# Two more waits inside GpSimd's row of gathers in a graph attention kernel on one core

## The chip, the core and the metric

The kernel runs on one core of a Trainium2 chip. The metric is the device time of one execution in microseconds (us); lower is better. The core has five engines that run side by side and meet through semaphores: TensorE (PE), VectorE (DVE), ScalarE (ACT), GpSimd (POOL) and SyncE (SP).

## The reference

Two layers of graph attention over a graph of 12500 nodes and 200000 edges, with the edges sorted by destination, and a self loop at each node:

```python
def _gat_layer(h_in, W, a_s, a_d, b, src, dst, n):
    h = (h_in @ W).reshape(n, Hh, Cc)                  # 4 heads x 64 channels
    alpha_s = jnp.sum(h * a_s, axis=-1)
    alpha_d = jnp.sum(h * a_d, axis=-1)
    e = jax.nn.leaky_relu(alpha_s[src] + alpha_d[dst], 0.2)
    m = jax.lax.stop_gradient(jax.ops.segment_max(e, dst, num_segments=n))
    ex = jnp.exp(e - m[dst])
    alpha = ex / jax.ops.segment_sum(ex, dst, num_segments=n)[dst]
    out = jax.ops.segment_sum(h[src] * alpha[:, :, None], dst, num_segments=n)
    return out.reshape(n, Hh * Cc) + b
...
h = jnp.maximum(_layernorm(x, axis=-1), 0.0)
h = gelu(_gat_layer(h, W0, ...)); h = gelu(_gat_layer(h, W1, ...))
return x + h
```

## The kernel before

A dense first part (up to about 170 us) normalises x, multiplies it by W0 and stores a table of rows in DRAM: for each node 264 numbers, four heads of 64 channels and two logits. It also lays the edge list out in chunks of 14 x 128 edges and works out on the chip how many steps there are.

The rest is 112 steps for each of the two layers, 224 in all. A step takes one chunk of 1792 edges and one window of 128 destination nodes. Its work is spread over five bodies of a software pipeline, so in each body five neighbouring steps are under way, each in another role:

- **GpSimd** brings the source rows of a step: 14 gathers (13 in the first 68 steps, where ScalarE makes the last column itself), each an indirect DMA of 128 rows of 1056 bytes into one column of the tile `rows_all` (buffer u of 4, L598 before the change). In front of a step's gathers it waits for `sum_done` of the step three before (L594) and for the step's edge list, `edge_landed` (L595). One group of instructions like this is one step for GpSimd; nothing else is on its queue after the dense part.
- **VectorE**, once a step's rows have landed (`landed`), copies the logits out (`take_values`, L1091), scans for maxima along the edges, and joins the scans across partitions with a carry from step to step (`scan_partitions`; the last operation, L1122, signals `carry_ready`). In the same body it finishes falls and weights of the step before (L1170 to L1183, L1081), compares edge destinations with the window to make one-hots (`one_hots_of_edges`, L1106, which signals `onehot_ready`), and finishes the nodes of the step two before (`node_shares`, `node_totals`, `node_means` up to L1201).
- **TensorE** turns carries round (L1321), spreads logits to edges (L1310) and sums the weighted rows by destination: `sum_up`, 14 products of 128x128 by 128x264 in fp32 (L1328; each stands as two passes, 28 rows of the trace a step). The last of them signals `sum_done`.
- **ScalarE** makes exponentials, weighs the last columns and stores results; **SyncE** loads edge lists, destination rows, marks and the nodes' own rows.

The order on each engine is written out by hand: the function `pipeline` calls the engine's body for each step, and semaphores that count steps hold the engines together. `t.done(1)` is the count that a semaphore has when the step before t is through; `t.done(3)` the one for three steps before. `nc.gpsimd.sem_inc(gathers_begun, 1)` only gives the wait an instruction to hang on.

Of the kernel before, what the change touches and what calls it, by code (L numbers as in the profile page):

```python
# [23 lines left out]
def two_layer_graph_attention(nc, x, src, dst, edge_attr, W0, a_src0, a_dst0, b0, W1, a_src1, a_dst1, b1, out):  # L24
# [44 lines left out]
    with ExitStack() as ctx:  # L69
# [3 lines left out]
        def sem(name):  # L73
            return ctx.enter_context(nc.semaphore(name))
# [184 lines left out]
        gathers_begun, aggr_begun, loads_begun = sem("gathers_begun"), sem("aggr_begun"), sem("loads_begun")  # L259
# [32 lines left out]
        s = {n: sem(n) for n in step_sems}  # L292
# [181 lines left out]
        def _(pool):  # L474
# [107 lines left out]
            for L in range(2):  # L582

                if L == 0:
                    pool.wait_ge(rows_stored[0], 16 * (GROUPS // 2 + 2))
                    pool.wait_ge(rows_stored[1], 16 * (GROUPS // 2))
                else:
                    pool.wait_ge(stored, (rounds_ + 1) * (16 * NB) + 16)
                    nc.gpsimd.sem_inc(gathers_begun, 1)
                def gather_round(r, counts, slots):  # L590
                    for u in range(NB):
                        t = Step(pool, L, r, rounds_, u, counts, slots < SLOTS)
                        pool.wait_ge(s["sum_done"], t.done(3))
                        pool.wait_ge(s["edge_landed"][u], t.landed(16))  # L594
                        nc.gpsimd.sem_inc(gathers_begun, 1)  # L595
                        index = edge[u][:, E_SRC, :].bitcast(I32)
                        for j in range(slots):
                            nc.gpsimd.indirect_dma_start(  # L598
                                out=G[u][:, j, :], out_offset=None, in_=table[L][0:N, :],
                                in_offset=bass.IndirectOffsetOnAxis(ap=index[:, j:j + 1], axis=0)).then_inc(s["landed"][u], 16)  # L600

                if L == 0:
                    with nc.gpsimd.Fori(0, AHEAD) as r:
                        gather_round(r, {}, SLOTS - 1)
                with nc.gpsimd.Fori(AHEAD if L == 0 else 0, rounds_ + 1) as r:
                    gather_round(r, {}, SLOTS)
# [815 lines left out]
```

## Time and profile before

| what | value |
|---|---|
| median of 3 runs (lowest, highest) | 4977.21 us (4950.52, 4978.08) |
| the profiled execution | 4959.4 us |
| its span in the trace | 4957.5 us |
| granted TensorE clock, mean over the span | 0.76 |
| first gather of a step, first and last step | 169.8 us and 4897 us |

The trace is of one execution, 1.9 us longer than its span. In it an instruction row of GpSimd's gathers is the time in which the engine makes the transfer's descriptors; the data lands later. "Idle before" on a row is the time in which the engine had nothing to show, with what the profile names as its end: "issue" is nothing that it sees, "remote" a semaphore whose giver it can't name. Waits, register operations and semaphore operations are not counted as busy and don't stand in the timeline; the view by source line has them.

### The profile page before, as it was taken

To read this page: it belongs to the slowest core of one execution; us is meant where nothing else is said; L and a number is where in the kernel's file an instruction comes from. 1 tells how busy PE (TensorE), PEld (TensorE's weight loads), DVE (VectorE), ACT (ScalarE), POOL (GpSimd) and SP (SyncE) were. 2 spreads that over 40 slices of the span, in tenths; PEclk is the share of its full clock that TensorE was granted. 3 is DMA by queue.
4 is the path that set the end of the run, shared out by engine and by line. 5 is a ranking of instruction groups with operands and counts; after the bars stand their busy time and mean duration, and the time that the engine had idled before them with its cause. 6 is when DMAs were issued, how large, how long until landed. Compare 5 with 4: busy or idle time off the path is not lost.

```text
span 4957.5 us, 58322 instructions
## 1 busy us (share of the span) xinstructions
PE 2920.6 (59%) x10195; PEld 1927.3 (39%) x10195; DVE 3692.9 (74%) x13203; ACT 2353.5 (47%) x7376; POOL 3054.6 (62%) x3215
## 2 busy tenths in 40 slices
PE   7467666677666555565545555555555555555555
PEld 6244444444444333343423333333333333333333
DVE  7577777878777677676757777777777777777777
ACT  5255555555555444444443444444444444444445
POOL 7566656666656655566546666666666666666664
PEclk9688888888788777777767777777777777777777
DMA  8444444444444444444434444444444444444443
GB/s 266 141 129 128 128 119 128 132 128 126 125 120 127 124 115 123 117 121 122 122 99 124 128 133 133 133 133 132 133 135 133 132 130 133 133 133 131 134 135 91
DMA packets 326730, 645.75 MB, mean 130 GB/s; under 512 B 97683, under 2 KB 195387, under 8 KB 326635
## 3 DMA queue, kind: packets, MB, share of 16 engines
q0 software_dynamic: 152224, 428.76, 32.5%
q1 hardware_dynamic: 128664, 172.56, 11.5%
q10 hardware_dynamic: 45746, 43.56, 2.6%
q14 instruction: 85, 0.69, 0.0%
q8 instruction: 11, 0.18, 0.0%
HBM read 596.90 MB, written 47.71 MB: 130 GB/s over the span
## 4 chain that ended last, share of the span: by engine, by line
DVE 70%; issue 14%; another core or an unknown queue 11%; PE 2%; ACT 1%; DVEq 1%; POOL 1%; DMA 0%; ACTq 0%; SPq 0%; POOLq 0%
DVE rows_all L1081 9%; DVE groups_or_hots L1106 9%; DVE stores_or_hots L1059 5%; DVE of_node L1162 3%; DVE vectors_or_means L1201 3%; DVE total L1188 3%; DVE node_logit L1160 3%; DVE node_l L1152 2%; DVE runs L1117 2%; DVE dloc L1103 1%; DVE stats_or_carry L1122 1%; DVE runs L1119 1%; DVE logit L1180 1%; DVE pre L1178 1%
## 5 line engine op out<-in xcount | busy, mean ns | idle before, releaser
L598 POOL DMA_INDIRECT rows_all<-table,edge x3068 | 2933.2, 956 | 1821.5 <-issue 953.7
L1328 PE MATMUL bank<-rows_all,groups_or_hots 128*128 128x264 f32 x6272 | 1783.3, 440 | 47.3 <-issue 23.0
L1328 PEld LDWEIGHTS bank<-rows_all,groups_or_hots 128*128 128x128 f32 x6272 | 1328.9, 219 | 452.6 <-issue 147.2
L1310 PE MATMUL bank<-stores_or_hots,logit_p 128*128 128x448 bf16 x896 | 368.8, 566 | 1314.6 <-DVE logit_p L1072 1142.0
L706 ACT ACTIVATE rows_all<-rows_all 128x64 f32<-128x64 f32 x3584 | 881.6, 341 | 3.7
L1310 PEld LDWEIGHTS bank<-stores_or_hots,logit_p 128*128 128x128 bf16 x896 | 98.9, 131 | 1513.0 <-DVE logit_p L1072 1214.7
L1081 DVE TENSOR_TENSOR rows_all<-rows_all,bank 128x768 f32<-128x768 f32 (+1 forms) x672 | 658.8, 1037 | 0.0
L1106 DVE TENSOR_TENSOR groups_or_hots<-bank,dloc 128x1792 f32<-128x1792 f32 x224 | 453.5, 2025 | 159.5 <-remote 101.2
L736 ACT ACT_TABLE_LOAD x224 | 287.4, 1283 | 400.2 <-issue 377.6
L718 ACT ACTIVATE share<-node_d 128x8 f32<-128x8 f32 x224 | 47.0, 210 | 694.5 <-DVE node_d L1155 550.7
L730 ACT ACTIVATE bank<-fall 128x56 f32<-128x56 f32 x224 | 49.6, 222 | 544.2 <-DVE fall L1183 357.8
L1201 DVE SCALAR_TENSOR_TENSOR vectors_or_means<-normed_or_dst,inv,bias 128x64 f32<-128x64 f32 x896 | 195.9, 281 | 145.3 <-remote 82.7
L1059 DVE TENSOR_SCALAR stores_or_hots<-normed_or_dst,node 128x448 bf16<-128x448 int16 x896 | 252.5, 342 | 50.4 <-remote 40.9
L730 ACT ACT_TABLE_LOAD x222 | 284.8, 1283 | 4.7 <-ACT row L744 0.7
L1315 PE MATMUL bank<-ident,ahead 128*4 128x128 f32 x224 | 81.9, 366 | 291.8 <-issue 167.6
L724 ACT ACTIVATE bank<-products_or_rows,share 128x64 f32<-128x64 f32 x896 | 233.5, 331 | 0.0
L1336 PE MATMUL bank<-total,heir 128*128 128x264 f32 x448 | 226.7, 606 | 0.8 <-DVE heir L1189 0.8
L721 ACT ACTIVATE vectors_or_means<-bank,share 128x65 f32<-128x65 f32 x896 | 209.2, 317 | 7.3
L736 ACT ACTIVATE bank<-vectors_or_means 128x256 f32<-128x256 f32 x112 | 43.4, 388 | 302.8 <-DVE vectors_or_means L1201 268.6
L1350 PE MATMUL bank<-w_ext,stores_or_hots 128*128 128x264 f32 x448 | 133.4, 423 | 84.1 <-ACT rows_all L699 44.3
L1315 PEld LDWEIGHTS bank<-ident,ahead 128*4 128x4 f32 x224 | 18.7, 83 | 420.4 <-issue 268.1
L1162 DVE TENSOR_REDUCE of_node<-node_logit 128x112 f32<-128x336 f32 x224 | 166.7, 744 | 11.2 <-DVE node_logit L1160 2.8
(192 smaller groups left out, 4054.9 us busy)
## 6 DMA issues: line engine op xcount, KB each, us to landing
normed_or_dst<-dst_row SPq DMA_DIRECT2D x224, 448.0 KB
rows_all<-table,edge POOLq DMA_INDIRECT x3068
products_or_rows<-table SPq DMA_DIRECT2D x224, 132.0 KB
table<-row ACTq DMA_DIRECT2D x112, 132.0 KB
early_or_lists<-in_x_dram SPq DMA_DIRECT2D x112, 128.0 KB
out_dram<-vectors_or_means ACTq DMA_DIRECT2D x112, 128.0 KB
table<-stores_or_hots ACTq DMA_DIRECT2D x24, 528.0 KB
groups_or_hots<-in_x_dram SPq DMA_DIRECT2D x24, 512.0 KB
```

What stands on the lines that cost most here:

```text
L598: nc.gpsimd.indirect_dma_start(out=G[u][:, j, :], out_offset=None, in_=table[L][0:N, :], in_offset=bass.IndirectOffsetOnAxis(ap=index[:, j ...
L706: last = nc.scalar.activation(G4[t.u][:, j, h, 0:C], G4[t.u][:, j, h, 0:C], ACT.Copy, scale=G4[t.u][:, j, h, C:C + 1])
L724: last = nc.scalar.activation(own_part[:, h, :], self_row[t.u][:, h * HW:h * HW + C], ACT.Copy, scale=share[:, 0, h:h + 1])
L730: nc.scalar.activation(edge_w.rearrange("p (t h) -> p h t", h=H), fall[:], ACT.Exp).then_inc(s["w_ready"], 1)
L736: nc.scalar.activation(act_o[t.half][:] if t.L == 0 else act_p, mean_o[:], ACT.Gelu).then_inc(s["act_ready"], 1)
L1059: last = nc.vector.tensor_scalar(flat[:, of], dst_b[t.half][:, of], node[:, 0:1], None, ALU.is_equal)
L1081: nc.vector.tensor_tensor(rows[:, :, 0:C], rows[:, :, 0:C], wide(edge_w[:, t0 * H:t1 * H], 2, C), ALU.mult).then_inc(s["weighted"][nth], 1)
L1106: nc.vector.tensor_tensor(onehot[t.half][:], wide(numbers, 1, SLOTS), wide(dloc[:], 2, P), ALU.is_equal).then_inc(s["onehot_ready"], 1)
L1162: nc.vector.tensor_reduce(of_node[:].rearrange("p k h t -> p (k h) t"), node_logit[:].rearrange("p (t c) -> p t c", c=SQ)[:, :, 0:6 * H].r ...
L1201: last = nc.vector.scalar_tensor_tensor(out=mean_o[:, h * C:(h + 1) * C], in0=summed[:, h, :], scalar=inv[:, h:h + 1], in1=bias[:, t.L, h ...
L1310: last = nc.tensor.matmul(bank[0][:, 0:SLOTS * SQ], logit_p[:, q * P:(q + 1) * P], of[:, q], start=(q == 0), stop=(q == QUADS - 1))
L1328: last = nc.tensor.matmul(bank[3 + t.half][:, 0:ROW], onehot[t.half][:, j, :], G[t.u][:, j, :], start=(j == 0), stop=(j == SLOTS - 1))
```

## The change

Inside a step's row of gathers, GpSimd waits twice more: in front of the 10th gather (j == 9) until VectorE has made the carries of the step before, and in front of the 13th (j == 12) until it has made the edge one-hots of the step before. Both hold in all 224 steps. Nothing else is changed, and no other engine has another instruction.

```diff
                         nc.gpsimd.sem_inc(gathers_begun, 1)
                         index = edge[u][:, E_SRC, :].bitcast(I32)
                         for j in range(slots):
+                            if j == 9:
+                                pool.wait_ge(s["carry_ready"], t.done(1))
+                                nc.gpsimd.sem_inc(gathers_begun, 1)
+                            if j == 12:
+                                pool.wait_ge(s["onehot_ready"], t.done(1))
+                                nc.gpsimd.sem_inc(gathers_begun, 1)
                             nc.gpsimd.indirect_dma_start(
                                 out=G[u][:, j, :], out_offset=None, in_=table[L][0:N, :],
                                 in_offset=bass.IndirectOffsetOnAxis(ap=index[:, j:j + 1], axis=0)).then_inc(s["landed"][u], 16)
```

GpSimd's queue over one step of 13 gathers and the start of the next, before the change (x12 means twelve such instructions in a row):

```order
L594 ISA [waits sum_done]
L598 DMA rows_all<-table,edge 128x264 [waits edge_landed0]
L598 DMA rows_all<-table,edge 128x264 x12
L593 REGISTER_ALU
L598 DMA rows_all<-table,edge 128x264 [waits sum_done,edge_landed1]
```

The same place after it:

```order
L594 ISA [waits sum_done]
L604 DMA rows_all<-table,edge 128x264 [waits edge_landed0]
L604 DMA rows_all<-table,edge 128x264 x8
L599 REGISTER_ALU
L604 DMA rows_all<-table,edge 128x264 [waits carry_ready]
L604 DMA rows_all<-table,edge 128x264 x2
L604 DMA rows_all<-table,edge 128x264 [waits onehot_ready]
L593 REGISTER_ALU
L604 DMA rows_all<-table,edge 128x264 [waits sum_done,edge_landed1]
```

No gather has moved against another one; the row of 13 (or 14) is now cut into 9, 3 and 1 (or 2), and the gathers' line number went from 598 to 604.

## Rows read from the trace of the kernel before

**Rows 1.** The page: span, busy times, the chain that ended last

```profile
span 4957.5 us, 58322 instructions
...
PE 2920.6 (59%) x10195; PEld 1927.3 (39%) x10195; DVE 3692.9 (74%) x13203; ACT 2353.5 (47%) x7376; POOL 3054.6 (62%) x3215
...
DVE 70%; issue 14%; another core or an unknown queue 11%; PE 2%; ACT 1%; DVEq 1%; POOL 1%; DMA 0%; ACTq 0%; SPq 0%; POOLq 0%
```

**Rows 2.** Source line 598 from 2600 to 4900 us; idle: us, times

```profile
L598 POOL DMA_INDIRECT rows_all<-table,edge x1527: 943/949/1547, 2599.7 to 4897.8; - x191
...
  issue: 455.4, 1418
  remote: 383.7, 109
```

**Rows 3.** Stages: GpSimd's gathers, busy us (count), clock, from 2600 to 4900 us

```profile
2600.00:4900.00 2300.00, 1459.93 (x1527) 0.72 0.47 132
```

**Rows 4.** Source line 598 from 250 to 1550 us

```profile
L598 POOL DMA_INDIRECT rows_all<-table,edge x845: 943/949/1545, 249.3 to 1542.3; - x169
```

**Rows 5.** Source line 598 from 1550 to 2500 us

```profile
L598 POOL DMA_INDIRECT rows_all<-table,edge x602: 943/949/1218, 1551.9 to 2497.4; - x151
```

**Rows 6.** Timeline of GpSimd, one step: start us, us, [idle before]

```profile
3592.98 0.95 POOL L598 DMA_INDIRECT rows_all<-table,edge  x1 [3.58 <-remote]
...
3604.26 0.95 POOL L598 DMA_INDIRECT rows_all<-table,edge  x1 [0.30 <-issue]
...
3608.02 0.94 POOL L598 DMA_INDIRECT rows_all<-table,edge  x1 [0.30 <-issue]
3609.27 0.94 POOL L598 DMA_INDIRECT rows_all<-table,edge  x1 [0.30 <-issue]
3613.88 0.95 POOL L598 DMA_INDIRECT rows_all<-table,edge  x1 [3.67 <-remote]
```

**Rows 7.** Timeline of TensorE, the end of the sum awaited there

```profile
3604.85 3.38 PE L1328 MATMUL bank<-rows_all,groups_or_hots 128*128 128x264 f32 x14
```

**Rows 8.** Source line 593 (the register operation behind the last gather), same step

```profile
L593 POOLq ALU_OP  x1: 32/32/32, 3599.1 to 3599.1; - x1
```

**Rows 9.** Source line 595 (the second step's wait), from 170 to 180 us

```profile
L595 POOLq EVENT_SEMAPHORE  x1: 43/43/43, 175.4 to 175.4; - x1
```

**Rows 10.** Timeline of GpSimd, the first four steps

```profile
184.84 0.95 POOL L598 DMA_INDIRECT rows_all<-table,edge  x1 [0.30 <-issue]
186.09 0.94 POOL L598 DMA_INDIRECT rows_all<-table,edge  x1 [0.30 <-issue]
...
249.27 0.95 POOL L598 DMA_INDIRECT rows_all<-table,edge  x1 [30.89 <-PE bank L1328]
```

**Rows 11.** Timeline of VectorE in the step of rows 6

```profile
3597.56 0.21 DVE L1091 COPY value<-rows_all 128x56 f32<-128x56 f32 x1
...
3602.26 0.41 DVE L1122 TENSOR_TENSOR stats_or_carry<-runs,lists_or_marks 4x256 f32<-4x256 f32 x1
...
3608.55 2.02 DVE L1106 TENSOR_TENSOR groups_or_hots<-bank,dloc 128x1792 f32<-128x1792 f32 x1 [1.81 <-remote]
```

**Rows 12.** Timeline of GpSimd, the last gather of layer 2's first step

```profile
2580.88 0.95 POOL L598 DMA_INDIRECT rows_all<-table,edge  x1 [0.30 <-issue]
```

**Rows 13.** Timeline of VectorE, the read that waits for that gather

```profile
2583.65 0.21 DVE L1091 COPY value<-rows_all 128x56 f32<-128x56 f32 x1 [17.05 <-DMA rows_all<-table,edge]
```

**Rows 14.** Groups of VectorE, 2600 to 4900 us: busy, mean ns | idle before

```profile
L1106 DVE TENSOR_TENSOR groups_or_hots<-bank,dloc 128x1792 f32<-128x1792 f32 x109 | 220.7, 2025 | 106.7 <-remote 71.6 <-DVE dloc L1103 21.8 <-issue 12.3
```

**Rows 15.** Timeline of VectorE in layer 1 at a loop's turn

```profile
1996.67 0.27 DVE L1170 TENSOR_TENSOR reach<-edge,bank 128x112 f32<-128x112 f32 x1 [4.30 <-issue]
```

**Rows 16.** Timeline of VectorE, the first two steps

```profile
228.97 0.41 DVE L1122 TENSOR_TENSOR stats_or_carry<-runs,lists_or_marks 4x256 f32<-4x256 f32 x1
229.56 2.02 DVE L1106 TENSOR_TENSOR groups_or_hots<-bank,dloc 128x1792 f32<-128x1792 f32 x1
...
236.70 0.20 DVE L1091 COPY value<-rows_all 128x56 f32<-128x56 f32 x1
241.35 0.41 DVE L1122 TENSOR_TENSOR stats_or_carry<-runs,lists_or_marks 4x256 f32<-4x256 f32 x1
```

## The prediction

> **What bounds the kernel now.** I read the page first. VectorE is 74% busy, GpSimd 62%, and the chain that ended last lies 70% on VectorE and 1% on GpSimd [rows 1]; that looks like a kernel bound by VectorE. The source line of the gathers tells another story. From 2600 to 4900 us GpSimd ran 1527 gathers, busy 1459.9 us [rows 3]; its idle time in front of them was 455.4 us in 1418 pieces and 383.7 us in 109 pieces [rows 2]. Together that is 2299.0 of the stretch's 2300 us: gathers and the two kinds of gap fill GpSimd's time. 1527 gathers are 109.1 steps of 14, so a step takes 21.09 us there. It is made of 14 gathers at 0.95 us with 0.30 us between two [rows 6], 17.5 us, a gap between two steps of 383.7 / 109 = 3.52 us in place of one 0.30, which gives 20.8, and some 0.25 us of rarer hiccups in the "issue" pieces. In the first 68 steps (13 gathers) a step takes 1300 us / 65 = 20.0 us [rows 4]; the same sum gives 13 x 1.25 + 3.2 = 19.5. From 1550 to 2500 us a step takes 950 / 43 = 22.1 us [rows 5], a full us over the sum: there VectorE sets the pace, with idle stretches such as 4.30 us in front of L1170 where its loop turns [rows 15].
>
> So the gap of 3.52 us matters more than the page says. What is it? In one step the last gather ends at 3609.27 + 0.94 = 3610.21, and the next step's first starts 3.67 us later [rows 6]. The sum it waits for ended at 3604.85 + 3.38 = 3608.23 by TensorE's rows [rows 7], two us before the gathers were through. A wait tested when its gather's turn comes would have passed for 0.30. The register operation written behind the step's last gather ran at 3599.1, 6.1 us after the first gather started, with nine gathers still to come [rows 8, 6]: GpSimd's sequencer hands out a gather each 6.1 / 14 = 0.44 us and stands at the next wait some 11 us before the queue is empty. At the program's start the semaphores are already high enough. There the second step's wait passed at 175.4, inside the first step's gathers [rows 9], and the gap between the two steps was 0.30 us [rows 10]. I read from this: **a wait that is met when the sequencer reaches it costs nothing; one that is unmet, even if it is met soon after, costs 3.2 us** (3.52 - 0.30), because the next gather then starts only some 3.5 us after the queued ones have ended.
>
> **The change part by part.** Both waits are priced in the step of [rows 6], counted from its first gather (3592.98).
>
> The wait for carries. Nine gathers are handed out in 9 x 0.44 us, less the 0.8 by which the sequencer leads the first one: it stands at the wait at about +3.2. The carries of the step before were done at 3602.67, which is +9.7 [rows 11]. Could they be done by +3.2? VectorE reads a step's logits 2.8 us after its last gather's start at the earliest [rows 12, 13], and carries come 5.1 us after that read (3597.56 to 3602.67) [rows 11]. With the smallest gap between steps, 0.30, the last gather starts at -1.25, so the carries are never there before +6.6. This wait is unmet in every step but the first of a layer: the 9th gather ends at +11.0, the 10th starts at +14.4 in place of +11.3. Price 3.2 us a step. Queued behind it are five gathers and the next step; waiting for these is VectorE's L1091 alone.
>
> The wait for one-hots. Three gathers later, at +13.7 + 3 x 0.44 = +15.0, the sequencer stands here. The one-hots were done at 3610.57, +17.6 [rows 11], in a step with 1.81 us idle in front of L1106; on average that idle is 106.7 / 109 = 1.0 us [rows 14]. That step would miss it. But VectorE has room to be earlier: it reads the logits at +4.6, and the bound above is +1.6. If it runs 3 us earlier, the one-hots come at +14.6 even there, and the wait is met.
>
> The old wait at the step's end. It used to be reached 11 us early. Now the sequencer gets there at +13.7 + 5 x 0.44, about +16. The sum for the next step ended at 3608.23, +15.3 [rows 7], and comes no later if VectorE is earlier. So it is met, and its 3.2 us **fall away**.
>
> The net of a step is 3.2 + 0 - 3.2: one unmet wait before, one after, in another place, 20.8 us before the hiccups as now. The third wait is the doubtful one: bounds are 0 (always met) and 3.2 us (always unmet); below nothing it can't go, since it takes no gather away. I take 0 because one miss shifts GpSimd 3.2 us later against VectorE, and the next step then meets it. Where VectorE sets the pace (22.1 us) a miss hides in the spare time.
>
> At the ends the cover is missing. Step 1's 10th gather used to run at 197; now it waits for carries at 229.38 and its 13th for one-hots at 231.58, unmet, so its data is there at about 240 in place of the read at 236.70 [rows 16]: +3.2. Step 2 starts at about 238, its 9th gather ends at 249.4, then 3.5 us and four gathers: the fourth step's first gather moves from 249.27 [rows 10] to about 258, +9 us in a stretch that GpSimd bounds. Layer 2's second and third steps, back to back today, lose 3.2 us each; a later wait for the sum may take up all of it or nothing (0 to 6), and since it follows within a step I take 2. Sum: 4957.5 + 9 + 2 = 4968.5 us of span, 4970 with the 1.9 us around it. The profiled execution is 18 us under the median of the runs, so on their scale it is 4977 + 11 = **4988 us**.
>
> A page weighed. In [rows 6] the gap stood although the sum was done two us before. The Trainium skill, GPSIMD Engine Reference, Instruction dispatch, says that completion gates what waits on an instruction's semaphore and does not hold back the next Pool instruction. By it a wait would cost only its lateness: carries at +9.7 are before the 10th gather's old turn (+11.3), so the change would cost nothing there; the row speaks against the rule as a price of waits.
>
> **The rivals.**
>
> *VectorE is held less, faster.* VectorE stands idle in front of small operations while GpSimd has gathers queued and stands at a wait, 1.0 us a step before L1106 alone [rows 14]. If a queue cut into 9, 3 and 2 shortens such stretches, what the steps take over GpSimd's sum comes back: 1.0 us of 22.1 in 43 steps [rows 5] and 0.5 of 20.0 in 65 [rows 4], 43 + 32 = 75 us. With the 11 of the ends: 4913 us; if the hiccups of 0.25 us go too (some 180 steps, 45 us), 4868. I take the middle, 4890. Against it: GpSimd's floor of 20.8 us stays. A page tells of such holding: by the Trainium skill, SBUF — State Buffer, Who interferes with whom, a VectorE operation with two SBUF inputs contends with GpSimd reads, one with at most one SBUF input outside the 2-port modes does not. L1106 reads one input in PSUM and waits 106.7 us all the same [rows 14], so the row and the rule differ, and I take no gain from it.
>
> *The one-hots are late in a share of the steps, slower.* It decides at one point: one-hots later than +15.0. The step of [rows 11] is 2.6 us over it. If VectorE, stalled in the stretch before GpSimd's release (now +3 to +13.7 instead of the step's last ten us), doesn't get earlier, the miss returns each time it has slipped again. One step in three: 75 x 3.2 = 240 us, 5228 us; one in eight 5080, two in five 5275.
>
> *Late in nearly every step, slower.* VectorE's own pace then rises with the stalls, to the 24.0 us of two unmet waits. 224 x 3.2 = 717: 5705 us. For it: scans and falls (L1091 to L1183) would stand in the stretch where idle now is. Against: a step of 24 us gives VectorE 3 us to catch up.
>
> *The waits do nothing.* Both met whenever reached: then the step's end pays as before, 4977 us. The bound of +6.6 against +3.2 speaks against it; it would fall into the first case's range.
>
> **How the numbers follow.** The first case, with the last one in it, 0.40, 4940 to 5025 us; faster 0.25, 4860 to 4925; a share of misses 0.20, 5050 to 5290; nearly all 0.15, about 5700. The likeliest gives 4988. The range has to leave out no more than 0.2: it goes from 4860 to 5290 and leaves out the double miss, and a little below and between. A measurement of this kernel tells some 1% from no change, 50 us (its runs spread by 28). Faster by more: 0.25; within: 0.39; slower by more: 0.36.
>
> **What would show it.** In the changed profile the gap between steps is 0.30, and one of 3.4 to 3.6 stands in front of each 10th gather: right for the first part. Gaps over 3 us in front of 13th gathers count the misses: 0 to 30 for the forecast, some 75 for the third case. VectorE's L1091 sits 1.6 to 3 us after the first gather of the next step, not 4.6. If the 10th gather starts at +11.3 in most steps, my price of an unmet wait is wrong; if the gaps stand in front of first gathers as well, the sum for the next step is late, and the time is over 5700. If VectorE's idle in front of L1106 falls below 0.5 us and the middle stretch under 21.5 us a step, the faster rival holds.

## The result and the profile after

The changed kernel takes **5104.16 us** (median of 4 runs, 5090.66 to 5112.16) beside 4977.65 us for the kernel before (4 runs, 4950.52 to 4979.86): a ratio of **1.0268**, 95% interval 1.0234 to 1.0301. The forecast was 4988 us, so 116 us too low. The time lies in the range, in the part that the rival "the one-hots are late in a share of the steps" had brought in; what happened is another thing than that rival, as shown below. The profiled execution has a span of 5096.4 us against 4957.5 [rows 1].

The page of the changed kernel: span and busy times, and the chain that ended last (shares of the span).

```profile
span 5096.4 us, 58882 instructions
...
PE 2903.2 (57%) x10195; PEld 1924.7 (38%) x10195; DVE 3705.3 (73%) x13203; ACT 2347.7 (46%) x7376; POOL 3041.2 (60%) x3215
...
DVE 70%; issue 14%; another core or an unknown queue 12%; PE 1%; POOL 1%; DVEq 1%; DMA 0%; ACT 0%; SPq 0%; ACTq 0%; POOLq 0%
```

VectorE is busy 12 us longer than before, the other engines are not; the page says nothing of where 139 us went. The source line of the gathers (now 604), from 2600 to 5030 us, does. Idle: us, times.

```profile
L604 POOL DMA_INDIRECT rows_all<-table,edge x1496: 943/949/1121, 2600.1 to 5026.1; - x187
...
  DVE groups_or_hots L1112: 568.9, 102
  issue: 410.1, 1345
  remote: 17.0, 5
  DVE stats_or_carry L1128: 13.4, 44
```

The 383.7 us in 109 gaps between steps [rows 2] are down to 17.0 in 5. The 102 pieces that VectorE's L1112 ends are new: 5.6 us each in front of the 13th gather, where the one-hots are awaited. The wait for the carries is named at 44 pieces of 0.30 us, the ordinary distance of two gathers. 2430 us for 1496 / 14 = 106.9 steps make 22.7 us a step, in place of 21.09.

The same line in layer 1's two stretches, for [rows 4] and [rows 5]:

```profile
L604 POOL DMA_INDIRECT rows_all<-table,edge x853: 942/949/1226, 249.8 to 1549.1; - x171
...
  issue: 247.4, 758
  remote: 162.2, 48
  DVE groups_or_hots L1112: 44.1, 20
  PE bank L1334: 24.2, 10
...
L604 POOL DMA_INDIRECT rows_all<-table,edge x600: 943/949/1182, 1549.1 to 2470.8; - x150
```

Here the kernel is faster: 853 gathers of 13 a step are 65.6 steps in the 1300 us that held 65, and 600 gathers (42.9 steps) now fit into 922.6 us, 21.5 us a step for 22.1. By the gathers' timeline layer 2's first gather starts at 2518.2 us for 2564.6 before, and the last step's first gather at 5035.1 for 4897.8. So the ledger is: layer 1 gives 46.4 us back, 111 steps of layer 2 cost 2516.9 - 2333.2 = 183.7 us, the tail 1.6, together 138.9. Of layer 1's 46.4 us, 10.8 are there when the fourth step begins (238.50 in place of 249.27).

A step of layer 2 in GpSimd's timeline, beside [rows 6]:

```profile
3595.70 0.95 POOL L604 DMA_INDIRECT rows_all<-table,edge  x1 [0.30 <-issue]
...
3605.73 0.95 POOL L604 DMA_INDIRECT rows_all<-table,edge  x1 [0.30 <-DVE stats_or_carry L1128]
3606.99 0.95 POOL L604 DMA_INDIRECT rows_all<-table,edge  x1 [0.30 <-issue]
...
3609.49 0.95 POOL L604 DMA_INDIRECT rows_all<-table,edge  x1 [0.30 <-issue]
3616.38 0.95 POOL L604 DMA_INDIRECT rows_all<-table,edge  x1 [5.93 <-DVE groups_or_hots L1112]
```

Count the rows: with the first gather at 3595.70, the one at 3605.73 is the 9th and the one at 3606.99 the 10th, the one that waits. The sequencer passed that wait at 3605.44, as the 8th gather ended, and the view names the carries at the next gather that started. Both stand 0.30 us behind the gather before them. The 13th is the one at 3616.38.

And what VectorE did in between, beside [rows 11] (L1128 makes the carries, L1112 the one-hots; L1137 to L1161 are `node_shares`):

```profile
3604.99 0.41 DVE L1128 TENSOR_TENSOR stats_or_carry<-runs,lists_or_marks 4x256 f32<-4x256 f32 x1
...
3605.87 0.16 DVE L1148 TENSOR_TENSOR least_max<-old_max,products_or_rows 128x4 f32<-128x4 f32 x1
3607.31 0.16 DVE L1150 TENSOR_TENSOR edge_max<-mean_max,absent 128x4 f32<-128x4 f32 x1 [1.28 <-DVE mean_max L1146]
...
3609.41 0.17 DVE L1153 TENSOR_TENSOR total<-edge_max,least_max 128x4 f32<-128x4 f32 x1 [1.87 <-remote]
...
3611.52 0.17 DVE L1156 TENSOR_TENSOR node_z<-total,products_or_rows 128x4 f32<-128x4 f32 x1 [1.83 <-remote]
3612.94 0.17 DVE L1158 SCALAR_TENSOR_TENSOR node_l<-node_z 128x12 f32<-128x12 f32 x1 [1.25 <-DVE node_z L1156]
...
3613.54 2.02 DVE L1112 TENSOR_TENSOR groups_or_hots<-bank,dloc 128x1792 f32<-128x1792 f32 x1
```

The first seven operations after the carries follow each other in 0.1 us. In the program these small operations wait for each other through semaphores. From here on each such wait takes 1.25 to 1.87 us: L1146 ended at 3605.95, and the trace has the rise of its semaphore at 3607.28. So it goes on until the last stall ends at 3612.94: 2.5 us after the last queued gather, 3609.49 + 0.95 = 3610.44. Only then come the one-hots. GpSimd holds back its 13th gather for the one-hots, and the one-hots, behind this chain, come only after GpSimd's queue has run dry. That is the circle.

### The profile page after: what moved, and what is told of

It reads as the page before. It is cut to its first block, busy times and chain, and to the rows that moved or that the text cites. A ratio compares the mean times of both kernels' runs of the same rounds, so it can differ in the third digit from the quotient of the medians.

```text
span 5096.4 us, 58882 instructions
## 1 busy us (share of the span) xinstructions
PE 2903.2 (57%) x10195; PEld 1924.7 (38%) x10195; DVE 3705.3 (73%) x13203; ACT 2347.7 (46%) x7376; POOL 3041.2 (60%) x3215
## 4 chain that ended last, share of the span: by engine, by line
DVE 70%; issue 14%; another core or an unknown queue 12%; PE 1%; POOL 1%; DVEq 1%; DMA 0%; ACT 0%; SPq 0%; ACTq 0%; POOLq 0%
DVE rows_all L1087 9%; DVE groups_or_hots L1112 9%; DVE stores_or_hots L1065 5%; DVE of_node L1168 3%; DVE vectors_or_means L1207 3%; DVE node_logit L1166 2%; DVE total L1194 2%; DVE node_l L1158 2%; DVE runs L1123 2%; DVE node_z L1156 2%; DVE dloc L1109 2%; DVE stats_or_carry L1128 1%; DVE runs L1125 1%; DVE edge_max L1150 1%
## 5 line engine op out<-in xcount | busy, mean ns | idle before, releaser
L1334 PE MATMUL bank<-rows_all,groups_or_hots 128*128 128x264 f32 x6272 | 1776.4, 439 | 48.6 <-issue 22.7
L1112 DVE TENSOR_TENSOR groups_or_hots<-bank,dloc 128x1792 f32<-128x1792 f32 x224 | 453.5, 2024 | 79.2 <-DVE dloc L1109 42.3
L1207 DVE SCALAR_TENSOR_TENSOR vectors_or_means<-normed_or_dst,inv,bias 128x64 f32<-128x64 f32 x896 | 195.5, 280 | 116.0 <-remote 65.6
L1156 DVE TENSOR_TENSOR node_z<-total,products_or_rows 128x4 f32<-128x4 f32 x224 | 37.2, 166 | 224.8 <-remote 211.9
L1158 DVE SCALAR_TENSOR_TENSOR node_l<-node_z 128x12 f32<-128x12 f32 x224 | 38.4, 171 | 205.7 <-remote 109.6
```

The lines of the kernel that those rows point to most:

```text
L1112: nc.vector.tensor_tensor(onehot[t.half][:], wide(numbers, 1, SLOTS), wide(dloc[:], 2, P), ALU.is_equal).then_inc(s["onehot_ready"], 1)
L1207: last = nc.vector.scalar_tensor_tensor(out=mean_o[:, h * C:(h + 1) * C], in0=summed[:, h, :], scalar=inv[:, h:h + 1], in1=bias[:, t.L, h ...
L1334: last = nc.tensor.matmul(bank[3 + t.half][:, 0:ROW], onehot[t.half][:, j, :], G[t.u][:, j, :], start=(j == 0), stop=(j == SLOTS - 1))
```

## The experiments

The first four ran on one chip, with the kernel before beside them at 4977.44 us (7 runs). Diffs are against the changed kernel unless said otherwise.

### Each wait alone

```diff
-                            if j == 12:
-                                pool.wait_ge(s["onehot_ready"], t.done(1))
-                                nc.gpsimd.sem_inc(gathers_begun, 1)
```

> Of the two waits only the one in front of the 10th gather (carries) is kept. Theory on record (R: each wait that is unmet when GpSimd's sequencer reaches it costs 3.2 us): carries' wait 3.2 us, and the wait at the step's end, reached at about +12 against a sum at +15.4, another 3.2 us: 24 us a step, about 5500 us. Theory A (the 10th gather waits only for what its data is late; the loss of the change comes from the one-hots' wait alone, which closes a circle in layer 2): the gap before the 10th gather stays at 0.3 us in most steps, the gap between steps is back at 3.5 us, layer 2 at 20.8 to 21.1 us a step, layer 1 as in the changed kernel or before: 4925 to 4980 us.

Measured: 4907.87 us, ratio **0.9854** (0.9822 to 0.9887). That is a little faster than theory A had it, and 590 us from theory R. Line 601 is that of its gathers, from 2600 to 4850 us:

```profile
L601 POOL DMA_INDIRECT rows_all<-table,edge x1499: 940/946/1548, 2599.9 to 4850.0; - x188
...
  issue: 442.9, 1382
  remote: 372.3, 107
  DVE stats_or_carry L1125: 3.0, 10
```

The wait for the carries costs nothing in layer 2: ten pieces of 0.30, and the gaps between steps are back (372.3 / 107 = 3.48 us). Its step there is 21.04 us, as before; layer 2's first gather stands at 2526.0 us, 38.6 earlier than before. The gain is all in layer 1.

```diff
-                            if j == 9:
-                                pool.wait_ge(s["carry_ready"], t.done(1))
-                                nc.gpsimd.sem_inc(gathers_begun, 1)
```

> Of the two waits only the one in front of the 13th gather (one-hots) is kept. R: it is reached at +4.5 and unmet in each step (3.2 us), the step's end is met: 20.8 to 21 us a step, about 4977 us. A: with twelve gathers in the queue VectorE's small dependent operations are held until some 2.6 us after the last of them, and the one-hots stand behind these: gap before the 13th gather 5 to 6 us in nearly each step of layer 2, 22.5 to 23 us a step there, 5060 to 5150 us in all.

Measured: 5190.61 us, ratio **1.0443** (1.0392 to 1.0495), 40 us above A's range. From 2600 to 5110 us:

```profile
L601 POOL DMA_INDIRECT rows_all<-table,edge x1552: 940/946/1168, 2603.1 to 5106.3; - x194
...
  DVE groups_or_hots L1109: 577.4, 103
```

The same 5.6 us as with both waits, and 22.71 us a step. What A had missed is layer 1: without the carries' wait the one-hots are late there too (206.2 us in 40 pieces between 250 and 1550 us), and the first stretch takes 20.9 us a step, where it took 19.8 with both waits and 20.05 with none. The whole loss of the change comes from the one-hots' wait, and the carries' wait softens it.

### Both waits in layer 1 only

```diff
-                            if j == 9:
+                            if L == 0 and j == 9:
...
-                            if j == 12:
+                            if L == 0 and j == 12:
```

> Both waits are there in layer 1's 112 steps and in none of layer 2's. R: about 4982 us (nothing but the start's loss). A: layer 1 keeps the 46 us that it gained in the changed kernel (first gather of layer 2 at about 2518 us in place of 2565), layer 2 takes 21.05 us a step as before: 4930 us, that is 0.990 of before.

Measured: 4925.31 us, ratio **0.9898** (0.9863 to 0.9934); layer 2's first gather at 2531.2 us, its steps 21.04 us. The ledger of the two traces holds when it is cut in two: layer 1 gains, layer 2 paid.

### The one-hots in front of the stalled chain

Both waits stay; on VectorE the order of two parts is exchanged, with one wait of VectorE's own added for the sum that holds the one-hots' buffer.

```diff
+                if landed:
+                    dve.wait_ge(s["sum_done"], landed.done(2))
+                    one_hots_of_edges(landed)
                 if finished:
                     node_shares(finished)
                 if landed:
-                    one_hots_of_edges(landed)
                     logits_of_edges(landed)
```

> Both waits as in the change; on VectorE the one-hots of the edges stand in front of the node shares (L1131 and following) in place of behind them, with a wait for the sum of two steps before, which holds their buffer. R: no difference from the changed kernel, or a little earlier one-hots, 4977 to 5104 us. A: the one-hots no longer stand behind six to eight small dependent operations that are held 1.2 to 1.9 us each while gathers are queued; they come at about +17.5 (2 us after the sum at +15.4) in place of +19.6, the gap before the 13th gather falls from 5.6 to about 3.5 us in layer 2 and a step there from 22.75 to some 20.8: about 4890 us. If the node shares then become late for ScalarE (it waits for their last result), the gain is smaller and stands as idle time there; a rival (B: what is late is the sum of two steps before, not the chain) would leave the gap at 5 us or more.

Measured: 4910.15 us, ratio **0.987** (0.9827 to 0.9914). The loss of 127 us is gone, turned into a gain of 67. One step, VectorE and then GpSimd:

```profile
3534.19 0.41 DVE L1128 TENSOR_TENSOR stats_or_carry<-runs,lists_or_marks 4x256 f32<-4x256 f32 x1
...
3534.96 2.02 DVE L1112 TENSOR_TENSOR groups_or_hots<-bank,dloc 128x1792 f32<-128x1792 f32 x1
...
3539.98 0.17 DVE L1158 SCALAR_TENSOR_TENSOR node_l<-node_z 128x12 f32<-128x12 f32 x1 [1.84 <-remote]
...
3540.24 0.95 POOL L604 DMA_INDIRECT rows_all<-table,edge  x1 [0.30 <-issue]
...
3546.04 0.95 POOL L604 DMA_INDIRECT rows_all<-table,edge  x1 [3.61 <-remote]
```

The one-hots are through at 3536.98, 11.8 us after the step's first gather in place of 19.6 us, and the 13th gather (3540.24) starts without a gap. The stalls still stand behind them (L1158) and hold nobody's gather. My expectation had two errors that cancelled in part: the sum that holds the one-hots' buffer is not the one at +15.4 but the one a step earlier, which is long done, so the one-hots came at 11.8 and not 17.5; but then the gap goes back to the step's end, 3.6 us, and a step still takes 21.05 us. The time of 4910 comes from layer 1, not from a step of 20.8. So the exchange shows that the loss sat in the chain in front of the one-hots; it doesn't show that the order is worth anything by itself, for the carries' wait alone gave 4907.87.

### What holds the step's end: the signal, not the wait

In the run with the carries' wait alone, a sum that ends by TensorE's row at 3544.13 + 3.38 = 3547.51 is taken by GpSimd's wait (L595) at 3553.0, with the queued gathers ended at 3550.21. The timeline of VectorE, TensorE and GpSimd:

```profile
3541.98 0.41 DVE L1125 TENSOR_TENSOR stats_or_carry<-runs,lists_or_marks 4x256 f32<-4x256 f32 x1
...
3544.13 3.38 PE L1331 MATMUL bank<-rows_all,groups_or_hots 128*128 128x264 f32 x14
...
3549.26 0.95 POOL L601 DMA_INDIRECT rows_all<-table,edge  x1 [0.30 <-issue]
3553.84 0.95 POOL L601 DMA_INDIRECT rows_all<-table,edge  x1 [3.63 <-remote]
```

The same stretch by source line, the two waits as they passed (L595 the sum's, L600 the carries'; duration ns, then first and last start):

```profile
L595 POOLq EVENT_SEMAPHORE  x1: 43/43/43, 3553.0 to 3553.0; - x1
...
L600 POOLq EVENT_SEMAPHORE  x1: 17/17/17, 3542.4 to 3542.4; - x1
```

The same engine, in the same step, took the carries' signal at 3542.4 within 0.05 us (L1125 ended at 3542.39). So an unmet wait has no price of its own as long as its signal comes while gathers are still queued. Where the queue is dry, the next gather starts 0.78 us after the wait has passed (3615.60 to 3616.38 in the changed kernel). The sum's signal is what comes late, 5.5 us after TensorE's row, and 2.8 us after the last queued gather. The semaphore records of the traces say so for `sum_done` itself: in ten steps from the 150th on it rises 19.9 to 21.1 us after the first gather in the kernel before, at 17.5 us in each of the ten in the changed one, where twelve gathers are queued and end near 14.8; the rows put the end of the sum at 13.3 to 16.2 in both. Over all of layer 2 the rise comes 3.6 to 7.5 us after the row's end in the kernel before. The ends of TensorE's rows are modelled, so these rows alone don't tell a late signal from a sum that ended late; that VectorE's semaphores are late in the same stretch, behind operations of 0.2 us, speaks for the signal. Four more runs were made to test it.

```diff
                             if j == 12:
-                                pool.wait_ge(s["onehot_ready"], t.done(1))
+                                pool.wait_ge(s["sum_done"], t.done(2))
```

> As the changed kernel, but the wait in front of the 13th gather is for another signal: the sum of the step two before, the one that the next step's first gather waits for anyway. By TensorE's rows this sum ends at +14.5 to +15.0, counted from the step's first gather, and twelve queued gathers end at +15.0. Theory S (the sum's signal, which the trace gives at +20.0 in the kernel before and at +17.5 in the changed one, reaches nobody until some 2.7 us after the last queued gather ended, whatever TensorE's rows say): the wait passes at +17.7, the gap before the 13th gather is 3.5 us, the gap between steps 0.3, a step of layer 2 takes 20.8 us as before, in all 4900 to 4930 us, as with the carries' wait alone. Theory T (the sum is signalled when TensorE's row ends, and what costs 3.2 us is the place at the end of a row of gathers): no gap over 1 us before the 13th gather, a step of layer 2 takes 18 to 20 us, 4600 to 4800 us in all.

Against the kernel before, with a shorter queue on GpSimd (`edge_step` is a semaphore of the dense part, `tick` a new tile of four columns):

```diff
                         for j in range(slots):
+                            if j in (5, 8, 11):
+                                pool.wait_ge(edge_step, done[0] + t.k * 4 + j // 3)
+                                nc.gpsimd.sem_inc(gathers_begun, 1)
                             nc.gpsimd.indirect_dma_start(
...
+                            if j in (2, 5, 8, 11):
+                                nc.gpsimd.memset(tick[:, j // 3:j // 3 + 1], 0.0).then_inc(edge_step, 1)
```

> The kernel before, without the change's waits; behind the 3rd, 6th, 9th and 12th gather GpSimd sets four bytes a partition, and in front of the 6th, 9th and 12th it waits until that operation three gathers earlier is done, so that never more than some five gathers are queued behind the running one. No gather waits for another engine that did not before. Theory Q (VectorE's small operations and the sum's signal are held because many gathers stand in GpSimd's queue): with the short queue the sum's signal passes at +15, the gap between steps falls from 3.5 to under 1 us, a step of layer 2 takes 18.5 to 20 us (14 x 1.25 and some 0.5 to 1 us for the four operations), 4700 to 4850 us in all. Theory P (they are held as long as gathers run one after another, however many are queued): gap between steps 3.5 us as before, plus the four operations: 21.3 to 22 us a step, 5000 to 5100 us.

> The kernel before, without the change's waits, with VectorE's one-hots of the edges in front of the node shares. If the gain of the run with both waits and this order (0.987) comes from the carries' wait, as the run with that wait alone (0.985) suggests, this order alone gives 4960 to 4990 us. If the order by itself is the gain, 4900 to 4930 us.

And both waits of the change for a step that is long through (`t.done(3)` in place of `t.done(1)`):

> Both waits are there, but for the carries and one-hots of the step three before in place of the last one, so both are met whenever GpSimd's sequencer comes to them. All theories: the four instructions a step cost nothing that can be measured, 4965 to 4990 us. If the mere instructions in the row of gathers brought layer 1's gain (they slow the sequencer down by a few tenths of a us a step), about 4930 us.

These four fell on another chip, and there **the kernel before itself takes 4144.83 us** (25 runs, 4140.47 to 4151.36), 833 us less than on the first. Measured against that, in the order above: 1.0106 for the sum awaited at the 13th gather (1.009 to 1.0123), 0.9996 for the short queue (0.9986 to 1.0005), 0.999 for VectorE's order alone (0.998 to 1.0) and 1.0001 for the two met waits (0.9992 to 1.0011). As tests of what they were made for they are void, except that the instructions of two met waits and four small operations a step cost nothing there. The order alone and the met waits were not run again on a chip like the first. Between S and T, or Q and P, they tell nothing: no gap over 1 us stood in layer 2 with any of the four kernels, whatever was changed, and a step took 17.6 us.

### The same kernels on other chips

> The changed kernel once more, unaltered, since the last four runs came from another chip than the first: there the kernel before takes 4145 us in place of 4977, and its sum's signal passes 0.01 us after TensorE's row has ended. Where the kernel before takes about 4977 us (signals held while gathers run one after another), the ratio should be that measured first, 1.027. Where it takes about 4145 us, the carries are there at +7.1 with nine gathers queued to +11.0, and the one-hots at +10.85 with twelve queued to +15: no gap in layer 2, and a loss only in the middle stretch of layer 1, where a step is late by the carries (13.0 instead of 7.1 at the most) every third or fourth time: ratio 1.000 to 1.012. By the rule on record (each unmet wait costs 3.2 us) the ratio there would be above 1.08, since no wait of the kernel before is unmet and long there.

> The kernel before with GpSimd's queue kept short, unaltered from the run before, for a chip on which signals are held. Theory Q (they are held because many gathers stand in the queue): gap between steps under 1 us, 18.5 to 20 us a step in layer 2, ratio 0.94 to 0.97 or less. Theory P (they are held as long as gathers run one after another, however many are queued): gap between steps 3.5 us, ratio 0.99 to 1.02. Where the kernel before takes about 4145 us this run tells nothing new: 1.000.

A third chip: the kernel before takes 5200.23 us there (7 runs). The changed kernel takes 5257.98 us, ratio **1.0124** (1.0061 to 1.0187). Layer 2 shows the same picture, 2700 to 5180 us:

```profile
L604 POOL DMA_INDIRECT rows_all<-table,edge x1492: 942/949/1126, 2699.1 to 5178.6; - x187
...
  DVE groups_or_hots L1112: 641.7, 106
```

That is 6.05 us a step and 23.3 us for the step. The short queue takes 5273.93 us, ratio 1.0172 (1.0108 to 1.0237), with a gap between steps of 5.2 us in the median: theory Q falls, and theory P's gap of 3.5 us was too small. One step's end in the timeline of GpSimd and VectorE:

```profile
3654.25 0.95 POOL L602 DMA_INDIRECT rows_all<-table,edge  x1 [0.30 <-issue]
3660.36 0.95 POOL L602 DMA_INDIRECT rows_all<-table,edge  x1 [5.16 <-DMA edge<-edges]
...
3655.04 0.16 DVE L1146 TENSOR_TENSOR mean_max<-bank,weight_r 128x4 f32<-128x4 f32 x1 [2.60 <-remote]
...
3657.17 0.16 DVE L1150 TENSOR_TENSOR edge_max<-mean_max,absent 128x4 f32<-128x4 f32 x1 [1.90 <-remote]
```

And there by source line, SyncE's issue of an edge list (L447) and GpSimd's wait at the step's end (L596):

```profile
L447 SPq DMA_DIRECT2D edge<-edges x1: 333/333/333, 3657.9 to 3657.9; - x1
...
L596 POOLq EVENT_SEMAPHORE  x1: 1372/1372/1372, 3658.2 to 3658.2; - x1
```

By the way the kernel is written, never more than some five gathers were queued, and VectorE's chain stalls all the same. SyncE issues the next edge list only at 3657.9, 2.7 us after the last gather ended (3655.20), and GpSimd then waits for that list as well. So a queue of five holds as one of twelve does: what is held goes with gathers that run one after another, as far as these two depths can tell.

> The carries' wait in front of the 10th gather and a wait for the next step's own sum in front of the 13th, unaltered from the run before, which fell on a chip that holds no signals. Where signals are held (the kernel before takes 4977 us or more): theory S (the sum's signal comes some 2.7 us after the last queued gather ended) gives a gap of 3.5 us before the 13th gather, 0.3 between steps and a layer 2 step as before, ratio 0.98 to 1.00; theory T (the place at the end of the row costs, not the signal) gives no gap in either place and a ratio under 0.96. Where none are held: 1.011, as before.

> The changed kernel, unaltered, for the third time, for the case that this chip holds no signals: ratio 1.000 to 1.012, no gap over 1 us in layer 2, some steps of the middle stretch late by their carries. Where signals are held: 1.01 to 1.03, with a gap of 5 to 6 us before nearly each 13th gather of layer 2.

These fell on a chip of the second kind (before 4146.39 us, 13 runs). The first gives 1.0078 (1.0062 to 1.0095): layer 2 takes 17.62 us a step as with the changed kernel, and the loss lies in layer 1, whose last 44 steps take 20.1 us each for 19.4. The changed kernel takes 4145.66 us, ratio **1.000** (0.9991 to 1.001). Its gathers from 2200 to 4080 us:

```profile
L604 POOL DMA_INDIRECT rows_all<-table,edge x1494: 942/947/1548, 2199.2 to 4079.8; - x187
...
  issue: 441.9, 1450
  PE bank L1334: 10.7, 35
  DVE groups_or_hots L1112: 1.5, 5
  DVE stats_or_carry L1128: 1.2, 4
```

TensorE's timeline, the end of a sum:

```profile
2985.94 3.38 PE L1334 MATMUL bank<-rows_all,groups_or_hots 128*128 128x264 f32 x14
```

The source line of the wait for it:

```profile
L595 POOLq EVENT_SEMAPHORE  x1: 43/43/43, 2989.5 to 2989.5; - x1
```

Every gap is the ordinary 0.30 us. The wait passed at 2989.5, 0.2 us after the sum's row ended (2989.32) and with four more gathers of the step still to come; here nothing is held. The carries come at 7.1 and the one-hots at 10.85 us after the first gather, before the 10th and 13th gathers' turns (11.3 and 15.0), so neither wait costs anything. Only in the middle stretch of layer 1 are the carries late in 10 steps (gaps of 2.0 to 4.2 us), and that hides in a stretch where other work sets the pace: 18.43 us a step with the change, 18.42 in the run with met waits.

Theory S against T, in the form of a run with the sum awaited at the 13th gather on a chip that holds signals, has thus not been run. S rests on the semaphore records above, in which `sum_done` itself rises late and GpSimd's wait passes within 0.03 us of the rise, and on the second kind of chip, where it rises 0.01 us after the sum's row.

## Why the prediction was right, and where it was not

That the time lies in the range is luck for the most part. The likeliest case, 4988 us, rested on two steps that both failed, and 5104 us fell into a part of the range that was there for another reason, misses in one step of eight to two of five.

- **What bounds the kernel**: right. GpSimd's gathers and their gaps fill layer 2, and its time moved with these gaps alone.
- **"A wait that is met when the sequencer reaches it costs nothing; one that is unmet, even if it is met soon after, costs 3.2 us."** This is the step that failed first. I read a rule for waits from one kind of wait. The carries' wait is unmet when reached (+3.2, the carries at +9.6 in most steps, as worked out) and the 10th gather starts 0.30 us behind the 9th all the same, at +11.3, which is the sign that the prediction had named for a wrong price. The 3.2 us belong to the sum's signal, which nobody gets until 2.7 us after the queue is dry.
- **Carries, 3.2 us a step**: measured 0 in layer 2 but for its third step; in 21 of the 108 steps of layer 1 from the fifth on the carries are late, and cost their lateness.
- **The page weighed**: by the Trainium skill, GPSIMD Engine Reference, Instruction dispatch, completion gates what waits on a semaphore and does not hold back the next Pool instruction. I said that the row spoke against it. The gap of 0.30 in front of the 10th gather, at 3606.99, agrees with it, and the sum's late signal does not contradict it; no run here shows why a signal is late. The 106.7 us in front of L1106 [rows 14], which I set against a rule on shared ports, are idle time before an operation and not a longer operation: it takes 2.02 us here as on a chip that holds nothing, so this row doesn't speak against that rule.
- **"If it runs 3 us earlier, the one-hots come at +14.6 even there, and the wait is met"**: this is the step that decided the sign. VectorE did not get earlier, it reads the logits at +4.3 (median) in layer 2, where the kernel before had +4.0, and between carries and one-hots it took 9.8 us where the rows of before had 4.4 in the median. The stalls that I put down to the stretch before the release lie, in the changed kernel, right between the two. The wait misses in 103 of 108 steps and costs 5.3 us each, not 3.2 in none.
- **The step's end falls away**: right, 0.30 us in 102 of 108 steps of layer 2, and worth 3.06 us a step. With the rarer hiccups before the second gather gone too (0.2 us), that leaves 5.0 - 3.1 - 0.2 = 1.7 us a step, which is 22.75 - 21.05.
- **The ends, +11 us**: wrong in sign. The fourth step's first gather moved from 249.27 [rows 10] to 238.50, not to 258. Before, the three first steps' gathers run without a break and VectorE's chain with them is held, for a gap of 30.89 us; the changed kernel's 13.89 us at the 10th gather (213.53) and 3.95 at 238.50 together are less. VectorE reads the first step's logits at 210.02 in place of 226.70. Layer 2's first four steps take 81.9 us in both kernels, so the 2 us put there were 0.
- **The rivals**: "VectorE is held less" came true in layer 1 (46 us of the 75 worked out there), "a share of misses" in layer 2, though as nearly every step and at a net price of 1.7 us in place of 3.2. "Nearly all" was the nearest in what happens and was priced at 717 us: it set the refund of the step's end against a price of the carries' wait that nobody pays, and it counted 3.2 us in layer 1's 112 steps as well, where the kernel got faster.

Which part of VectorE's stalls gives layer 1 its gain isn't shown (11 of the 46 us are won before the fourth step): the run with the carries' wait alone and the one with the exchanged order have it (38.6 and 45.6 us by layer 2's first gather), and on the chips that hold nothing there is no such gain. That it comes from breaks in the row of gathers that let VectorE's chain through is argued, not tested.

## What to carry to other kernels

A wait is priced by when its signal arrives where it is awaited; compare the row that ends the work with the row of the wait that passes, for each pair of engines, before taking a gap for the price of a wait. Before making engine A wait for B inside a row of A's work, look at whether B's way to that signal leads through the stretch that A's own work slows down; if it does, move the signal's operation in front of the slow chain (here from 1.027 to 0.987, with one wait of VectorE's own added), or wait for an earlier signal. Run a change of this size on more than one chip: the same edit gave 1.027, 1.012 and 1.000.

## What the hardware showed that was not expected

- The same program takes 4145, 4977 or 5200 us on different chips, each chip's runs within about 1%. In layer 2 a step of the changed kernel takes 22.75 or 23.3 us on the slower ones and 17.63 us on the fastest, with gathers of 0.95 us and 0.30 between them on all.
- On the slower chips, from some 10 us after a row of gathers began (13 with the exchanged order), small operations of VectorE that depend on each other stand 0.5 to 2.6 us each in most cases (0.1 us otherwise), and TensorE's `sum_done` rises up to 7.5 us after its row in the kernel before; where it is late, it does so 2.0 to 3.3 us after the last gather queued has ended. VectorE's signals to GpSimd took 0.05 us in such rows: the carries at +9.6 and, with the exchanged order, the one-hots at +10.5 to +12.6. Five queued gathers are enough for it.
- It is not signals alone. SyncE's own small instructions are drawn out too. The same instruction of the changed kernel, behind the load of a value (duration in ns: least, median, most), first on the slower chip, then on the fast one:

```profile
L439 SPq SEQ_ASSERT  x107: 6/691/1397, 2601.0 to 5024.5; - x107
...
L439 SPq SEQ_ASSERT  x107: 18/18/18, 2203.5 to 4073.1; - x107
```

- Those drawn out take about 0.70 or 1.40 us there, the first ones some 4 us after the row began. Whether the sequencer is slow or its records are, these rows don't tell, and whether taking the records has a part in it wasn't tested; the profiled execution took 5098.2 us, inside the 5090.66 to 5112.16 of all four. What begins the holding, and what differs between the chips, stays open; TensorE's granted clock differs with them (in the mean of the kernel before 0.76 and 0.74 on the slower ones, 0.81 on the fast ones), which doesn't by itself explain a late signal of VectorE.
- A wait of GpSimd with gathers queued behind the running one passes without draining them: 0.30 us between the gathers on either side, in all but one step of layer 2.
